# Attention maxima: rows sent out on ScalarE's DMA queue, and TensorE's wait for them placed behind two units of maxima and the fifth product

## The reference, cut to what matters

```python
attn = jnp.einsum('bnd,bmd->bnm', q * scale, k)          # 12 heads of 16, windows of 14 x 14
attn = (attn.reshape(-1, ws, ws, ws, ws) + rel_h[:, :, :, :, None]
        + rel_w[:, :, :, None, :]).reshape(-1, N, N)
attn = jax.nn.softmax(attn, axis=-1)                     # needs a maximum per query
out = (attn @ v)
```

## Time and profile before

| | |
|---|---|
| median of three runs | 738.89 us (737.77 to 743.34) |
| the profiled execution's own time | 742.52 us |
| its span, first to last instruction | 740.7 us |
| mean granted TensorE clock | 0.842 of full speed |
| TensorE matmuls busy | 625.7 us (84%) |
| VectorE, ScalarE, GpSimd busy | 327.9, 220.7, 134.6 us |

### The profile page before, as it was taken

One profiled execution on the slowest core, in us unless ns is written; L12 is line 12 of the kernel. 1 busy time (PEld: TensorE's weight loads), 2 busy tenths in 40 slices (PEclk: granted clock), 3 DMA queues, 4 the chain that ended last, 5 costly groups with the idle time before them and its releaser, 6 DMA issues.

```text
span 740.7 us, 13578 instructions
## 1 busy us (share of the span) xinstructions
PE 625.7 (84%) x4592; PEld 503.3 (68%) x4593; DVE 327.9 (44%) x946; ACT 220.7 (30%) x554; POOL 134.6 (18%) x113
## 2 busy tenths in 40 slices
PE   0499999999779698799999998987249999999992
PEld 0377886756547465566666886966249999999991
DVE  4344435458567564571112263535603334443431
ACT  1012322324233223322223142141114444444440
POOL 6020100510000000000000004224313333333332
PEclk9989965557686655799999999988569999999997
DMA  2722585835163371077000001003122233323221
GB/s 83 162 65 59 155 198 111 189 96 82 27 97 59 46 110 35 10 268 308 1 0 1 1 1 44 16 28 124 59 61 39 43 44 45 45 43 43 43 38 17
DMA packets 32969, 53.63 MB, mean 72 GB/s; under 512 B 6458, under 2 KB 26484, under 8 KB 31410
## 3 DMA queue, kind: packets, MB, share of 16 engines
q1 hardware_dynamic: 24962, 43.51, 24.7%
q0 software_dynamic: 7968, 9.60, 7.6%
HBM read 32.95 MB, written 20.29 MB: 72 GB/s over the span
## 4 chain that ended last, share of the span: by engine, by line
PE 68%; SPq 8%; DVE 8%; DMA 6%; issue 4%; ACT 2%; POOL 2%; DVEq 0%; ACTq 0%; POOLq 0%
PE ps L1631 10%; PE ps L1617 7%; PE ps L1622 5%; PE ps L1462 4%; PE ps L1324 4%; PE ps L1184 4%; PE ps L1185 3%; PE ps L1450 3%; PE ps L1315 3%; DMA x<-in_xp 3%; PE ps L1519 2%; PE ps L1361 2%; PE ps L1604 2%; POOL xs_d L552 2%; PE ps L1454 2%
## 5 line engine op out<-in xcount | busy, mean ns | idle before, releaser
L565 POOL DMA_INDIRECT out<-ys,place_i x39 | 66.9, 1715 | 125.3 <-DVE ys L1161 70.9
L1631 PE MATMUL ps<-w2e,hts 128*128 x468 | 82.7, 327 | 1.5 <-DVE ys L1161 1.5
L1631 PEld LDWEIGHTS ps<-w2e,hts 128*128 128x128 f32 x468 | 75.1, 190 | 1.9 <-issue 1.8
L1324 PE MATMUL ps<-qa,ka 48*98 48x196 f32 x384 | 61.6, 457 | 8.1 <-ACT pt L634 5.9
L552 POOL DMA_INDIRECT xs_d<-rows,slot_i x32 | 31.5, 986 | 190.6 <-DVE slot_i L1073 182.0
L871 DVE TENSOR_REDUCE negm<-ps 98x2 f32<-98x392 f32 x96 | 49.1, 553 | 37.9 <-PE ps L1279 37.7
L741 ACT ACTIVATE hts<-ps,wst 128x128 f32<-128x128 f32 x234 | 64.5, 382 | 2.2 <-PE ps L1622 2.2
L634 ACT ACTIVATE pt<-ps 98x392 f32<-98x392 f32 x96 | 42.5, 494 | 66.7 <-PE ps L1324 66.7
L1617 PE MATMUL ps<-xst,wst 128*128 128x128 f32 x468 | 60.0, 279 | 1.1 <-ACT xst L574 1.1
L1617 PEld LDWEIGHTS ps<-xst,wst 128*128 128x128 f32 x468 | 58.4, 195 | 1.7 <-issue 1.7
L879 DVE RECIPROCAL rsum<-ps 128x128 f32<-128x128 f32 x48 | 42.3, 923 | 30.3 <-PE ps L1361 30.3
(11 more groups left out here) (212 smaller groups left out, 1024.6 us busy)
## 6 DMA issues: line engine op xcount, KB each, us to landing
w1e<-in_w1e SPq DMA_DIRECT2D x8, 579.0 KB, 10.2
w2e<-in_w2e SPq DMA_DIRECT2D x8, 576.0 KB, 11.1
xs<-xs_d SPq DMA_DIRECT2D x39, 98.0 KB, 1.9
ka<-k_d SPq DMA_DIRECT2D x12, 170.0 KB
k_d<-kst SPq DMA_DIRECT2D x16, 121.5 KB, 1.9
x<-in_xp SPq DMA_DIRECT2D x4, 384.0 KB, 20.2
q_d<-qt SPq DMA_DIRECT2D x2, 768.0 KB, 5.5
qa<-q_d SPq DMA_DIRECT2D x12, 128.0 KB
```

What stands on the lines that cost most here:

```text
L565: nc.gpsimd.indirect_dma_start(acc, bass.IndirectOffsetOnAxis(ap=place_i[:, j % 2:j % 2 + 1], axis=0), ys[:, j % 2, :], None, compute_op=A ...
L1324: last = mm(ps[0:98, banks[e], k * WIN:(k + 1) * WIN], ka[head(e), n, key_cols(b) + 98 * k:key_cols(b) + 98 * k + 98], qa[head(e), n, b * ...
L1631: last = mm(ps[:, 5, 0:D], hts[:, u, k, :], w2e[:, ds(e, 1), k, :], start=(k == 0), stop=(k == HT - 1))
```

## The change

`max_rows` is taken out of SP's stream, with its calls. Its four DMAs are issued by ScalarE at the end of `turn_max`, behind a wait for ScalarE's own two copies. In TensorE's `pair`, `lb` is still waited for first. The waits for `v_pair`, `lf` and `m_in` come after maxima units 0 and 1, and the fifth product of the pair before is moved ahead of them, and so ahead of the first scores.

```diff
-            def max_rows(p, n):
-                sp.wait_ge(s["m_row_ok"], 2 * p + 2)
-                for e in range(2):
-                    ...
-                    sp.dma_start(row, mrow[8 * e:8 * e + 8, n, :]).then_inc(s["m_in"], 16)
...
-            max_rows(0, 0)
...
-            def pair_step(p, n, more, rows=True):
+            def pair_step(p, n, more):
                 if more:
                     sp.wait_ge(s["m_ps"], 20 * p + 20)
                     load_pair(p + 2, n, 1)
-                if rows:
-                    max_rows(p + 1, 1 - n)
                 sp.wait_ge(s["o_ok"], 1 + 2 * p + 2)
...
                 nc.scalar.activation(erow[:, n, :], ps[0:8, MAX_BANKS[2], 2 * P:3 * P], ACT.Copy).then_inc(s["m_row_ok"], 1)
+                act.wait_ge(s["m_row_ok"], 2 * p + 2)
+                for e in range(2):
+                    r = e * HALF + AUG - 1
+                    row = qa[r:r + 1, n, :].rearrange("o (b t) -> o b t", b=NIMG)[:, :, 0:WIN]
+                    act.dma_start(row, mrow[8 * e:8 * e + 8, n, :]).then_inc(s["m_in"], 16)
+                    row = qa[r:r + 1, n, :].rearrange("o (bp par t) -> o bp par t", bp=NIMG // 2, par=2)
+                    act.dma_start(row[:, :, :, WIN:],
+                                  erow[4 * e:4 * e + 4, n, :].rearrange("p (par t) -> p par t", par=2)[:, :, 4:]
+                                  ).then_inc(s["m_in"], 16)
...
                 more = not last
-                pe.wait_ge(s[f"lf{n}"], itp * 128 + 128)
-                pe.wait_ge(s["m_in"], 64 * p + 64)
-                pe.wait_ge(s["v_pair"], 2 * p + 2)
                 if more:
                     pe.wait_ge(s[f"lb{1 - n}"], (itp + n) * 128 + 128)
...
                     for mu in mus[:2]:
                         max_unit(p + 1, 1 - n, mu)
+                    if j == 0:
+                        if not first:
+                            product(p - 1, 1 - n, 4)
+                        pe.wait_ge(s["v_pair"], 2 * p + 2)
+                        pe.wait_ge(s[f"lf{n}"], itp * 128 + 128)
+                        pe.wait_ge(s["m_in"], 64 * p + 64)
                     score_units(p, n, j)
...
-                    if j == 0 and not first:
-                        product(p - 1, 1 - n, 4)
```

More of the change, by code:

```diff
@@ L347, in load_pair @@
                                          rel_d[low][kind][ds(WS * e + 2 * WS * p, WS), :]).then_inc(sq, 16)
-            def max_rows(p, n):
-                sp.wait_ge(s["m_row_ok"], 2 * p + 2)
-                for e in range(2):
-                    r = e * HALF + AUG - 1
-                    row = qa[r:r + 1, n, :].rearrange("o (b t) -> o b t", b=NIMG)[:, :, 0:WIN]
-                    sp.dma_start(row, mrow[8 * e:8 * e + 8, n, :]).then_inc(s["m_in"], 16)
[L356 to L359, removed]
             store_rels(0)
```

## The result

The changed kernel takes 742.34 us at the median of 20 executions, the kernel before 737.81 us over as many: a ratio of 1.0063 (95% interval 1.0036 to 1.0091), or 4.5 us slower. Beside later experiments on another chip it was 1.0073 (1.0041 to 1.0105). A ratio leaves out executions more than 1.5% above the fastest of the same kernel; the medians are over all of them. The profiled execution has a span of 744.5 us against 740.7.

The account below looks back on a forecast made before the run. Pairs 2 and 3 were taken as bound by a loop through VectorE, SP and the DMA engines, not TensorE's work. Delays of 1.8 + 1.8 = +3.6 us on the median 738.9 gave 742.5, taken as 742; range 735 to 750.

Parts of the forecast that it names:

- the twin: Starts of pairs 2 to 4: bf16 loads finish moving when the rows do, so the wait for `lb` stays.
- the delay by ScalarE's issues: Four row issues ahead of exponential 14 delay it by 1.8 us in pairs 0 and 4, 2.5 in pair 1.
- Rows off SP's queue: SP's batch end: removing 2.85 us of issue before SP's wait for `ot` moves nothing SP issues: 0.
- ScalarE's issues: 2.85 us for four: ScalarE's queue: four row DMAs take 2.85 us together, some 0.7 us each, as on SP.
- Pairs 1 to 3 hide the stall: Ends of pairs 1 to 3: the 2.5 us delay fits in the idle before the next start: 0.
- The clock rival: Adverse side: stall at `j` = 8 lowers the clock, tail 2.1 us longer; up to 744.5; chance 0.2 for either sign.
- The product ahead of the first scores: TensorE's pair start: product and first scores swap places, `ot` keeps its 11.3 us: 0.
- Pair 4: +1.8: ScalarE's issues end at 279.4 against exponential 14 at 277.60; pair 5 starts behind exponentials, so +1.8 us is on the path.
- Clock stays up: Shorter waits keep TensorE's clock up: 2.2 us off each such period, 738 to 740; chance 0.2 for either sign.

Follow-up runs that it names:

- the experiment with the product back: Changed kernel with the fifth product moved back behind the first scores, waits for rows staying late: 743.95 us, 1.0086 to the kernel before.
- the experiment with two issues on either side: Changed kernel with two row DMAs in front of exponential 14 and two behind exponential 15: 1.000 (0.996 to 1.004) to the kernel before.
- early loads and rows spread: Changed kernel with SP's loop written out, float32 loads early, two row DMAs behind exponential 15 and two behind 17: 716.13 us, 0.9577 to the kernel before.

## Why the prediction was right, and where not

The forecast of 742 us, no change within 1% but a little slower, holds; so do the twin and the delay by ScalarE's issues. The account behind the number was partly different: two steps were off, in opposite directions, and the closeness is in part luck.

- *The twin.* Right. With the rows left on SP it appears whole, 14.6 us instead of 14.1; in the changed kernel only 0.46 us of it is seen, because ScalarE's stall has used up the idle in front.
- *Rows off SP's queue: 0.* Right. With TensorE's new order the rows measured 0.9984 on SP and 0.9973 on ScalarE behind exponentials 15 and 17.
- *ScalarE's issues: 2.85 us for four.* Right: 0.65, 0.66, 0.65, 0.66 and gaps, 2.7 us. The four ahead of pair 0 cost nothing, as forecast: from TensorE's table matmuls to the first scores of pair 0 it is 7.6 us before and after (121.72 to 129.31, 121.36 to 128.93). Idle at `j` = 8 grew from 0.58 to 2.40 at half clock (1.8, as forecast) and to 3.08 at full clock (2.5, as forecast). In pair 0 the 1.8 show as 1.4 (156.89 - 155.45), since the pair starts 0.4 us earlier in this trace.
- *Pairs 1 to 3 hide the stall: 0.* This step failed: their ends slip by 0.9, 1.2 and 0.6 us, 2.8 in all. The clock rival had foreseen a slip (a tail 2.1 us longer, 1.0 past the slack in pairs 1 and 2), but it came in two parts. In pair 1 the tail from the scores of `j` = 8 to the end took 3.9 us instead of 2.55 (188.43 to 192.29, 183.40 to 185.95), 1.3 longer. And the way from the start to `j` = 8 took 27.1 us instead of 23.5, which is 1.1 more than the stall's 2.5: some 0.3 by the order of the product (next point), and the rest goes with a full clock that comes 17.8 us behind the start instead of 15.9 (179.1 - 161.33, 175.8 - 159.89). In all that is 4.9 us for an idle of 3.96. Pairs 2 and 3 repeat it, with 5.2 for 4.02 and 6.3 for 6.10. I had given 0.2 to effects of the clock over 1.5 us. Where the loads are early and no slack is left, they are the larger part: a pair takes 30.9 us with the stall and 23.3 to 26.3 without, and of that difference the stall itself is 2.5.
- *The product ahead of the first scores: 0.* Wrong by a third of a microsecond a pair, which the experiment with the product back confirms. The product used to cover exponential 0; now the second scores stand idle for 0.33 us behind it (197.55), and the product itself stands 0.64 us behind the last exponentials. From the start of pair 2 to the store of `ot` it takes 12.7 us (192.29 to 205.02), not 11.3. But the same order brings about 7 us back against the old one when rows are on ScalarE (741.73 against 748.62). Why pairs in the old order stayed at the half clock is open; it is no mark of that order alone, since pair 4 of the kernel before and a pair of the version with the rows behind exponentials 15 and 17 did so too, without the stall.
- *Pair 4: +1.8.* In the profiled executions it was -1.9: the pair took 33.2 us before (283.86 - 250.66) and 31.3 after. The stall is the same, but the kernel before ran all of that pair at half clock and the changed kernel did not. Nothing in the forecast had this, and one trace does not tell how often the kernel before does it: in the traces of three near relatives (rows on SP with the new order, rows behind 15 and 17, SP's loop written out) pair 4 reaches the full clock. So the sum was 1.4 + 2.8 - 1.9, then 0.8 in pair 5 (24.45 us to its last product instead of 23.69) and 0.7 behind it, together 3.8. Against the forecast of 3.6, which was 1.8 + 0 + 1.8, that closeness is in part luck.
- *Clock stays up.* The favourable side did not come in the changed kernel. Nor does a shorter stall keep the clock up: it falls behind one of 1.72 us as well, in the experiment with two issues on either side. More full clock came where no long stall was left in a pair, with early loads and rows spread.

## What to carry to other kernels

Ask of a wait at the start of a stage which other transfers end at the same moment: the bytes still moving when the named one was already issued are the twin, and moving the named wait wins nothing. A DMA issue is not free on an engine that stands between two stages of a pipeline: put it where that engine is idle, behind the last work someone waits for, and not in front of it. Slack that is counted at one clock may not be there once the clock falls behind the stall or rises later in front of it. And before two traces are compared pair by pair, see which pairs ran at which clock in each: one pair was worth 5 us here.

## What was unexpected of the hardware

- Four DMA issues on ScalarE's queue cost as much as on SP's, 0.65 to 0.68 us each. The very first on that queue took 1.24 us.
- With TensorE's new order and a stall of 3.1 us at `j` = 8, pairs 1 and 2 take 30.9 to 31.1 us in three traces, with some 10 us of full clock in a pair, whether the loads are late or early. Without the stall the same work was done in 23.3 to 26.3 us a pair.
- The granted clock fell after 10 us at full behind a stall of 3.1 us, after 9.6 us behind one of 1.72 us, and after 16.7 us with no idle over 0.87 us. What brings it down is open.
- Writing out SP's loop of two rounds, with nothing else changed, gave 0.9% (0.991, 0.9866 to 0.9955). Some 1.2 us a pair of it (0.7 to 1.7 by batch) are seen on SP's queue; the rest was not traced.
